# A new order of additions and of the second layer in a fused two-layer attention kernel

## The reference

```
x = x + layer0(gn(x))
    qkv = x @ w_qkv, split into q, k, v and into 4 units of 32 channels, dilations 1, 2, 4, 8
    per unit, 2 heads of 16 channels, per position:
      attn = softmax over the 9 neighbours of (q . k[neighbour]) * 16**-0.5
      out  = sum over the 9 neighbours of attn * v[neighbour]
    gate = softmax(mean(x) @ w_gate.T + b_gate) ; out[unit] *= gate[unit]
x = x + layer1(gn(x))
    p = W_qkv @ x + b_qkv ; 4 heads of 32 channels; q = k = v = p
    att = softmax(p p^T * 256**-0.5) (32 x 32 per head) ; out = W_proj @ (att p) + b_proj
```

## Time and profile before

| | us |
|---|---|
| median of 3 runs (lowest, highest) | 83.04 (82.88, 83.13) |
| the profiled execution | 83.13 |
| its span, first to last instruction | 81.3 |
| busy in it: TensorE, VectorE, ScalarE, GpSimd | 71.1, 67.5, 29.3, 41.5 |

### The profile page before, as it was taken

How to read it: one execution, slowest core, us unless ns; L and a number is a source line. 1 busy time by engine, 2 the same in 40 slices (tenths; PEclk the granted TensorE clock), 3 DMA queues, 4 the chain that set the end, 5 groups by cost and what they waited for, 6 DMA issues and landing times.

```text
span 81.3 us, 2474 instructions
## 1 busy us (share of the span) xinstructions
PE 71.1 (87%) x1010; PEld 51.4 (63%) x1010; DVE 67.5 (83%) x184; ACT 29.3 (36%) x92; POOL 41.5 (51%) x84
## 2 busy tenths in 40 slices
PE   4999998799995698999969797879999999999950
PEld 4999753466742466776857664567676868575530
DVE  2152999999999989999999699889999888597850
ACT  1762765963384000000030003230994271764200
POOL 7104018912930037999999999699990005100000
PEclk9999999999999999999999999999999999999999
DMA  1980055000000000000000000000000000012253
GB/s 27 315 286 18 0 120 142 7 0 8 0 0 4 0 12 0 0 0 4 8 0 0 0 0 0 8 0 0 0 0 8 0 0 12 0 57 72 73 194 129
DMA packets 2796, 3.06 MB, mean 38 GB/s; under 512 B 352, under 2 KB 2400, under 8 KB 2784
## 3 DMA queue, kind: packets, MB, share of 16 engines
q1 hardware_dynamic: 2496, 2.63, 10.5%
q10 hardware_dynamic: 288, 0.26, 0.9%
HBM read 1.84 MB, written 1.05 MB: 36 GB/s over the span
## 4 chain that ended last, share of the span: by engine, by line
DVE 54%; PE 28%; POOL 7%; issue 5%; ACT 2%; POOLq 0%
PE ps L815 27%; DVE qk L602 18%; DVE pv L643 12%; POOL rstd L342 3%; POOL acc L379 3%; DVE acc L655 3%; DVE pv L655 2%; DVE x L674 2%; DVE prob L622 2%; DVE smax L609 2%; DVE ssum L619 2%; POOL pv L379 2%; DVE sums L570 1%; DVE acc L643 1%; PE ps L972 1%
## 5 line engine op out<-in xcount | busy, mean ns | idle before, releaser
L815 PE MATMUL ps<-prob,sel 64*128 64x192 f32 (+6 forms) x192 | 17.8, 313 | 2.7 <-DVE pv L643 1.6
L643 DVE TENSOR_TENSOR pv<-ps,v 128x128 f32<-128x128 f32 (+7 forms) x32 | 17.1, 567 | 1.8 <-PE ps L815 0.8
L815 PEld LDWEIGHTS ps<-prob,sel 64*128 64x128 f32 x192 | 13.7, 186 | 6.9 <-DVE pv L643 3.5
L815 PE MATMUL ps<-xn,wp 128*32 128x256 f32 (+1 forms) x208 | 17.1, 384 | 0.9 <-ACT q L417 0.7
L815 PE MATMUL ps<-idle 128*128 128x128 f32 x82 | 14.6, 328 | 1.1 <-DVE idle L533 1.1
L379 POOL TENSOR_TENSOR pv<-pv 128x240 f32<-128x240 f32 (+3 forms) x24 | 14.1, 600 | 0.5 <-DVE pv L643 0.5
L815 PEld LDWEIGHTS ps<-idle 128*128 128x128 f32 x82 | 12.6, 231 | 2.4 <-DVE idle L533 1.1
L342 POOL TENSOR_TENSOR rstd<-gvar,mhalf 128x2 f32<-128x2 f32 (+1 forms) x6 | 4.9, 809 | 15.9 <-DVE gvar L549 15.9
L379 POOL TENSOR_TENSOR acc<-acc,pv 128x256 f32<-128x256 f32 (+4 forms) x20 | 12.7, 640 | 0.5
L815 PEld LDWEIGHTS ps<-xn,wp 128*32 128x32 f32 (+1 forms) x208 | 8.7, 116 | 6.1 <-ACT xn L443 1.3
L602 DVE TENSOR_TENSOR qk<-q,k 128x672 f32<-128x672 f32 (+7 forms) x21 | 11.4, 607 | 0.0
(11 more groups left out here) (82 smaller groups left out, 89.6 us busy)
## 6 DMA issues: line engine op xcount, KB each, us to landing
out_dram<-x SPq DMA_DIRECT2D x8, 128.0 KB, 1.8
gx<-x_dram SPq DMA_DIRECT2D x2, 256.0 KB, 4.4
gx<-x_dram ACTq DMA_DIRECT2D x2, 128.0 KB, 3.1
sel<-selc_dram SPq DMA_DIRECT2D x4, 64.0 KB, 2.2
wp<-wpack_dram SPq DMA_DIRECT2D x1, 194.0 KB, 4.2
gx<-x_dram SPq DMA_DIRECT2D x1, 192.0 KB, 2.8
wp<-wpack_dram SPq DMA_DIRECT2D x1, 131.0 KB, 2.2
gx<-x_dram SPq DMA_DIRECT2D x1, 128.0 KB, 3.0
```

What stands on the lines that cost most here:

```text
L643: last = nc.vector.tensor_tensor(o, a, b, ALU.mult)
L815: return nc.tensor.matmul(o, w, m, start=start, stop=stop)
```

## The change

- VectorE forms all products of units (1,1), (1,2) and (1,3) before it adds anything. Both first residuals of phase 0 come right after the first product of unit (1,1).
- Unit (1,2): VectorE adds within the three columns only, six additions (`COLUMN_STEPS`), the three columns' chains side by side. TensorE adds the three column sums while restoring.
- Unit (1,3): VectorE adds nothing; TensorE adds all nine products.
- `sum_second` is cut in two: `sum_first_part` (units (1,0) and (1,3)) and `sum_second_part` (units (1,1) and (1,2)). Phase 0 is restored in one block on 32x32 tiles.
- The variance's second and third instruction read PSUM in place of `gst`, with the sign turned in the addition.
- `nbias` of groups 0 and 1 is computed on GpSimd (`norm_bias` below is GpSimd's), behind the power; the first power stands two additions later.
- Norm (2,1) moves from ScalarE to VectorE. The order of the second layer is new on all four engines; seven of the late `keep_clock` matmuls go.

```diff
-NORMS_ON_DVE = ((2, 0), (3, 0), (3, 1))
-NORMS_ON_ACT = ((0, 0), (0, 1), (1, 0), (1, 1), (2, 1))
+NORMS_ON_DVE = ((2, 0), (2, 1), (3, 0), (3, 1))
+NORMS_ON_ACT = ((0, 0), (0, 1), (1, 0), (1, 1))
+COLUMN_UNIT = 2
+COLUMN_STEPS = ((4, 3), (1, 0), (7, 6), (4, 5), (1, 2), (7, 8))
-RSQRT_AFTER = ((1, 0, 4), (1, 1, 0))
+RSQRT_AFTER = ((1, 0, 6), (1, 1, 0))
...
+            def norm_bias(n, bs):
+                pool.wait_ge(rstd_ready, n + 1)
+                nc.gpsimd.tensor_tensor(nbias[:, bs], gst[:, bs, 0], rstd[:, bs], ALU.mult).then_inc(nbias_ready, 1)
...
                             rsqrt(PHASES + g, group(g))
+                            norm_bias(PHASES + g, group(g))
...
-                link(nc.vector.tensor_tensor(gsq[:, bs], gst[:, bs, 0], gst[:, bs, 0], ALU.mult))
-                nc.vector.scalar_tensor_tensor(out=gvar[:, bs], in0=gst[:, bs, 1], scalar=EPS, in1=gsq[:, bs],
-                                               op0=ALU.add, op1=ALU.subtract).then_inc(var_ready, 1)
+                link(nc.vector.tensor_tensor(gsq[:, bs], stats[:, :, 0], gst[:, bs, 0], ALU.mult))
+                nc.vector.scalar_tensor_tensor(out=gvar[:, bs], in0=stats[:, :, 1], scalar=EPS, in1=gsq[:, bs],
+                                               op0=ALU.add, op1=ALU.add).then_inc(var_ready, 1)
...
+            def add_column(n):
+                s, (onto, slot) = COLUMN_UNIT, COLUMN_STEPS[n]
+                dve.wait_ge(pv_ready, 12 + 3 * (s + 1))
...
+                o = rect(acc[:, 1, s, :] if onto == 4 else pv[s][:, onto, :])
+                if n >= 3:
+                    dve.wait_ge(dve_added, n - 2)
+                nc.vector.tensor_tensor(o, o, rect(pv[s][:, slot, :]), ALU.add).then_inc(dve_added, 1)
...
+            def add_tiles(ph, tiles, stop, finished=False):
+                for s, slot in tiles:
...
+                    for j in range(SLOTS):
+                        rows = slice(32 * j, 32 * j + 32)
+                        last = mm(view(ps, 512 * (BANK[GROUPS // PHASES * ph] + j) + at, dims, 32 * s, 32),
+                                  ident[rows, rows], view(t, first + at, dims, 32 * j, 32),
+                                  start=slot == 4, stop=(s, slot) in stop)
...
+            def restore():
...
+                whole = [(s, 4) for s in range(ND)]
+                add_tiles(0, whole, whole, finished=True)
+
+            def sum_first_part():
+                s = LAST_UNIT
                 pe.wait_ge(pv_ready, 12 * PHASES)
+                pe.wait_ge(added, ADDS * POOL_SUMS[0] + ADDS)
+                add_tiles(1, [(0, 4)] + [(s, slot) for slot in (4, 3, 5, 1, 0, 2, 7, 6, 8)], [(0, 4), (s, 8)])
+
+            def sum_second_part():
                 pe.wait_ge(added, ADDS * sum(POOL_SUMS))
-                pe.wait_ge(dve_added, ADDS)
...
+                pe.wait_ge(dve_added, len(COLUMN_STEPS))
+                s = COLUMN_UNIT
+                add_tiles(1, [(1, 4), (s, 4), (s, 1), (s, 7)], [(1, 4), (s, 7)], finished=True)
```

More of the change, by code:

```diff
@@ L493, in _ @@
                 norm(0, i)
[L494 to L498, removed]
+            copy_projection(0, 0)
+            norm(1, 0)
+            copy_projection(0, 1)
+            norm(1, 1)
             for i in range(2):
                 copy_pT(0, i)
+            attention_exp(0)
+            copy_projection(1, 0)
+            squares(2)
+            copy_fused(0, 1)
             copy_projection(1, 1)
+            squares(3)
             for i in range(2):
                 copy_pT(1, i)
-            attention_exp(0)
             attention_exp(1)
[L506 to L511, removed]
             for g in range(2, 4):
@@ L514, in _ @@
                     copy_projection(g, i)
-            copy_pT(3, 0)
+            for i in range(2):
+                copy_fused(1, i)
+            for i in range(2):
+                copy_pT(3, i)
             attention_exp(2)
-            copy_pT(3, 1)
             attention_exp(3)
@@ L644, in multiply_pv, with rect @@
                 last.then_inc(pv_ready, 1)
[L646 to L666, removed]
-                    nc.vector.tensor_tensor(o, o, a, ALU.add).then_inc(last_added, 1)
+            def add_column(n):
+                s, (onto, slot) = COLUMN_UNIT, COLUMN_STEPS[n]
+                dve.wait_ge(pv_ready, 12 + 3 * (s + 1))
+                ci, ri = divmod(slot, 3)
+                r0, r1 = valid_rows(s, ri)
+                c0, c1, _ = columns(DIL[s], ci)
+                def rect(t):
+                    return t.rearrange("p (r c) -> p r c", c=W)[:, r0:r1, c0:c1]
+                o = rect(acc[:, 1, s, :] if onto == 4 else pv[s][:, onto, :])
+                if n >= 3:
+                    dve.wait_ge(dve_added, n - 2)
+                nc.vector.tensor_tensor(o, o, rect(pv[s][:, slot, :]), ALU.add).then_inc(dve_added, 1)
             def first_residual(g):
@@ L788, in _ @@
             second_variance(2)
-            attention_divide(1)
             second_variance(3)
             second_norm_bias(2)
-            norm(2, 0)
+            for i in range(2):
+                norm(2, i)
+            attention_shift(1)
             second_norm_bias(3)
@@ L795, in _ @@
                 norm(3, i)
-            copy_pT(2, 0)
+            attention_divide(1)
             second_residual(0, 0)
-            copy_pT(2, 1)
+            for i in range(2):
+                copy_pT(2, i)
             second_residual(0, 1)
@@ L1090, in _ @@
             for i in range(2):
-                project_second(2, i)
-            transpose(2, 0)
-            project_second(3, 0)
-            transpose(2, 1)
-            project_second(3, 1)
+                transpose(3, i)
             attention(2)
             for i in range(2):
-                transpose(3, i)
-            finish(1, 0)
+                finish(1, i)
             attention(3)
-            finish(1, 1)
             for i in range(2):
```

110 lines of the change are left out of this document (46 added, 64 removed).

## The result

The changed kernel took 81.93 us in the median of five executions, the kernel before 82.91. The ratio is 0.985 (95% interval 0.980 to 0.989), and timed once more beside the experiments it was 0.986 (0.983 to 0.989): faster by 1 to 2%.

What follows compares the result with a forecast made beforehand. VectorE was taken to bound 58.46 to 66.5 us, then mostly TensorE. A lead of 1.7 us at the residuals of groups 2 and 3, half given back in the tail, left 0.88: 83.04 - 0.88 = 82.2 us, range 81.5 to 83.2.

Steps and rivals of the forecast that it cites:

- Products first: Second layer up to 58 us: VectorE's products all end at 58.15 us, before at 63.2.
- waits for spreads: VectorE before products of unit (1,3): waiting for TensorE's spreads costs it 0.25 and 0.5 us.
- Variance from PSUM: VectorE's variances: reading PSUM saves 0.4 us, taken whole, bounds 0 and this sum.
- nbias on GpSimd: Biases of groups 0 and 1: the move saves VectorE 0.7 us and costs GpSimd 2 x 0.28.
- Restoring on small tiles: Phase 0 on TensorE: one block of 16 matmuls gives TensorE 1.4 us back, VectorE nothing.
- The additions: 58 to 65 us: fewer VectorE additions, 10 to 6, at 0.72 us beside GpSimd; the last two end at 62.0.
- Part one and part two: TensorE's sums: 2.25 us, hidden up to about 0.2, then 1.4 us from 62.05 to 63.45.
- price of 2.2 ns a column: TensorE's part one: rate read from 24 earlier matmuls, 1.41 us for 640 columns, giving 2.25 us.
- lead: Residuals of groups 2 and 3 start 1.7 us earlier, at about 63.4, bounds 0.6 and 2.3.
- The tail: After those residuals: group 1's work gives back half of the lead, leaving a gain of 0.88 us.
- The third rival: Group 3's squares on ScalarE do not wait for two copies: 0.7 us more kept, 81.5 us, chance 0.10.
- The clock: Rival: seven idle matmuls go, the clock falls for 2 us of work, costing 2 us: 84.2, chance 0.02.

Runs made afterwards that it cites:

- e11: e2 with the variance's second and third instruction reading gst in SBUF again: 0.988 of the kernel before.
- e8: e2 with nbias of groups 0 and 1 on VectorE and spread (1,3,0) ahead of projection 0,0 on TensorE: 0.991 of the kernel before.
- e4: The changed kernel with nbias of groups 0 and 1 back on VectorE: 1.006 of the kernel before.
- e3: The changed kernel with phase 0 restored by wide matmuls contracting all 128 partitions, in one block of 16: 0.989 of the kernel before.
- e9: e7 with two of VectorE's six additions moved into its waits among the products: 0.983 of the kernel before.
- e5: e2 with eight additions of unit (1,2) on VectorE, not six, TensorE adding only the finished sum: 0.990 of the kernel before.
- e10: e2 with all six additions of unit (1,2) behind product (1,3,0), undoing only products first: 1.041 of the kernel before.
- e7: e2 with group 3's squares ahead of two ScalarE copies and its group sums ahead of transpose 1,1 on TensorE: 81.39 us, 0.982 of the kernel before.
- e2: The changed kernel with three more idle matmuls behind the group sums of groups 0 and 1: 0.989 of the kernel before.
- e6: e2 with both parts of TensorE's sums together, behind the attention of group 0 and projection 1,0: 0.987 of the kernel before.
- e12: e2 with group 1's projection, transposes, attention, copies and shift ahead of the residuals again: 82.69 us in the one execution that kept its clock, no ratio.
- e1: The changed kernel timed again without an edit: 0.986 of the kernel before.

## Why the prediction was right, and where it was not

- **Products first.** Predicted 8.6 us after the first residual, measured 8.7. The waits for spreads were predicted as 0.25 and 0.5 and were 0.64 and 0.41. The first is larger for two reasons: the projection in front of that spread took 0.63 us from start to start and not 0.5, and VectorE came there 0.24 earlier, mostly because the two variances took 0.49 and 0.46 and not 0.6 and 0.55. The errors nearly cancelled; that is luck.
- **Variance from PSUM, 0.4 us of VectorE.** The excess went, as said; its worth is 0 (e11). I had taken the whole sum because VectorE had no idle time there before. After the change it has: the waits for the spreads, which the prediction itself had put at 0.25 and 0.5, could have swallowed the 0.4.
- **nbias on GpSimd.** Counted as 0.7 us of VectorE; worth 0.4 as such (e8), and 1.6 if TensorE's queue is left as it is (e4). The mechanism was named (the projections stand in the queue of the spreads) and not priced.
- **Restoring on small tiles.** Nothing for VectorE in the prediction; 0.3 us by e3, through TensorE.
- **The additions.** Here the reason was wrong in part and the sum right. I said that what is saved is the number of additions, and that part one is "hidden up to about 0.2 us". e9 shows that ending four of them 0.9 us earlier brings nothing while TensorE comes to the shift no sooner; e5 shows that eight cost what six cost, once TensorE gives up the two it had. What counts is that all products are done early (e10, at least 2.5 us). The time came out because both engines ended together, as the prediction had it within 0.2 us, and because both were over-priced by about as much (next point).
- **Part one and part two.** 2.25 and 1.4 us predicted, 1.92 and 1.33 measured. The price of 2.2 ns a column was too high for part one, which came to 1.9; why, is not shown, and TensorE's rows show no idle time in the 24 matmuls that it was read from. VectorE's four additions beside GpSimd took 2.49 us (57.69 to 60.18) and not 2.9. The two together give 0.26 more lead: 1.9 us for 1.7; with only one of them shorter the shift would have waited for the other engine.
- **The tail.** Half was to be given back, and 0.7 of 1.9 was. The squares ended 0.15 better than priced: I added durations of records that overlap (0.24 + 0.47, where the starts are 0.15 and 0.37 apart in the chain). These 0.15 and the 0.26 of the point before, less 0.1 that was lost between the fuses of group 2 and the end, make the 0.3 us by which 1.2 exceeds 0.88. The third rival, in which the squares do not wait for the two copies, did not come true: the copies are on the chain. Its size was 0.7 us; e7, which puts the squares first, gets 0.4.
- **The clock.** Given 2 in 100, and looked for in the tail. The kernel fell into this case in four of eleven executions, at 53.5 us and not in the tail, and it costs 4.6 us there and not 2. The prediction compared with a stretch of the kernel before, 1.15 of 2.00 us busy at full clock, and that was no guide: the stretch before the fall was fuller, 2.08 of 3.00. Work that restoring no longer takes from TensorE, counted there as a gain, is what e3 puts back to keep the clock; two of the seven idle matmuls that went had also stood in the middle, at 55 to 57 us, and not in the tail. An execution of the changed kernel at 86 us is slower than any of the kernel before that kept its clock. For the time in seven of eleven executions the forecast holds; for a kernel that must hold it, e2's three matmuls or e7 belong in it.

The move of norm (2,1) to VectorE was not undone by itself, nor were the seven idle matmuls put back where they were; what these two are worth stays open. Neither was e6 joined with e9. By e6's rows it should bring nothing more there: part two starts at 61.72, directly behind part one, and VectorE has ended at 61.56.

## What to carry to other kernels

When two engines end a stretch within a few tenths of each other, price the change on both and let the chain of waits decide which one it names; a saving on the other buys nothing (e9, e11). Before an instruction is moved to a cheaper engine or a later place, look at what stands behind its consumer in an in-order queue: that is its price (0.2 us of nbias, 1.6 us of time). Work taken off TensorE leaves gaps, and here gaps had a second price in the clock (4.6 us in four of eleven executions, for a gain of 1.2), so read the spread of the executions and the granted clock beside the median.

## What the runs showed of the hardware

- The granted clock fell to 1.2 GHz after TensorE had been busy 2.08 of 3.00 us, in some executions and not in others of the same kernel (four of eleven), and came back after about ten. The Trainium skill (TensorE: Matmul & The Clock Gate, "Part 1: The HAM clock gate (the "warmup" mystery)") has activity release the throttle and idleness bring it back; the runs agree in that more work in the gaps prevented the fall (none in 48 executions of e2, e3, e5 to e9 and e11). Its fall came here without any single gap above 0.51 us in the seven us before it.
- In e10 and e4 single gaps of 3.21 and 1.14 us went before the fall, in six of six and seven of twelve executions. e4 has the unfilled stretch of the changed kernel in front of its gap as well. In e12 the clock fell in five of six, in the profile at 68.5 us, 1.9 us behind the end of a gap of 1.11. In e10 and e12 it came back after about three us.
- The idle matmuls at a kernel's start took 4.15 to 5.06 us for the same 22, and the first residual of phase 0 starts 0.48 us later behind the longer one. Executions of one kernel that kept their clock differ by 0.2 to 0.6 us in e1 to e9, the 177.75 us left out; that this start explains most of it is likely and not shown, since one execution of each was profiled.
- A VectorE addition with both inputs in SBUF waits out a GpSimd addition: alone it records 0.34 us, beside GpSimd they come 0.67 to 0.70 apart. GpSimd's own come 0.63 apart alone and 0.73 beside VectorE's (e1).
- The variance's last instruction took 0.55 and 0.60 us beside GpSimd with both inputs in SBUF (e11), and 0.16 with one of them in PSUM.
- Small matmuls on 32x32 tiles can begin before others that were written ahead of them, by their recorded starts (61.85 against 62.31 in the profile of the changed kernel).
